# The loads of the residual tile move from SP's queue to ScalarE's, in the output-projection stage of an attention and expert layer

## The chip, the cores and the metric

One Trainium2 chip, eight of its cores. Every core runs the same program on one of the eight sequences (2048 tokens of 1024 numbers); the cores do not exchange data. The time is the device time of the slowest core, in microseconds (us).

## The reference

Two sublayers, each with a layer norm ahead of it and one behind it, and a residual added:

```python
x = x + _layernorm(_L0_attn_ref(_layernorm(x, axis=-1), Wq, Wk, Wv, Wo, ...), axis=-1)
x = x + _layernorm(_L0_ffn_ref(_layernorm(x, axis=-1), router_w1, router_w2, w1, w2, w3), axis=-1)
```

The first is differential attention: eight heads, each with two score matrices, O = (softmax(Q1 K1) - lambda softmax(Q2 K2)) V, an RMS norm of O per head, and `jnp.einsum('bne,de->bnd', O, Wo)`, a projection from 2048 to 1024. The second has 16 experts. Each picks the 256 tokens of the sequence with the highest router probability, computes w3 (silu(w1 x) * (w2 x)) and scatters the weighted results back. The inputs and outputs are float32; the kernel computes its matmuls in bf16.

## The kernel before

The program has five instruction streams, written out in order by a helper, `Plan`: `t` for TensorE, `v` for VectorE, `s` for ScalarE (ACT), `g` for GpSimd and `y` for SyncE (SP). `prod` appends an instruction that raises its engine's counter. `need(e, token)` appends a wait of engine `e` for another engine's counter (L79), but only if `e` has not already waited for that count or a higher one (L77). `dma(q, ...)` appends a load or store to the stream of engine `q` (L85); it is issued when that engine's program arrives at it. `need_dma` waits for the semaphore of a group of transfers (L90). `join_all` makes every engine wait for all others and for all transfers.

The stages, one behind the other and parted by `join_all`: layer norm and transpose of x with attention, head by head (L305 to L572); the output projection with residual and both norms (L576 to L693); the router and the choice of tokens; the experts (loads of w1, w2, w3 in float32, casts, three matmul groups for each of 64 chunks); the scatter with the last norm.

The change is in the output projection. Attention has left its result, transposed, in DRAM (`sc_ot`, 2048 x 2048 bf16), and the transposed Wo in `sc_wot`. SP first issues 16 loads that bring all of Wo to `s_woT` (L585, 256 KB each). Then a loop over `qc`, four blocks of 512 tokens:

- SP issues 16 loads of 128 KB into `s_otq[par]` (L599), one of two buffers. A row of a partition is 512 bf16 values, 1 KB.
- SP issues four loads of 512 KB of the kernel's input x into `s_x4` (L603), each a token tile of 128 x 1024 float32, so rows of 4 KB. There is one `s_x4` buffer; L601 asks that the adds of the block before have read it.
- TensorE waits for the block's `s_otq` loads (L604) and for no others, and does 8 groups of 16 matmuls (L612). VectorE copies each group to `s_ao4` (L622).
- VectorE takes mean and variance (L629 to L638), ACT makes 1/sqrt from it by Ln and Exp (L641, L644), VectorE applies them (L649, where it also waits for the x4 loads, L647, and for the x2 stores of the block before, L648) and adds `s_x4` (L655). The token of the adds is `x4_used`.
- SP waits for the four adds (L659) and stores the sum x2 to DRAM, four stores of 512 KB (L661).
- VectorE and ACT do the second norm (L666 to L684), with its result kept in `s_x2n`. ACT waits for the statistics (L677) ahead of L678, and has nothing behind L681 until L641 of the next block.

SP goes through this in program order. In block `qc + 1` its loads therefore stand behind the stores of block `qc`, and so behind L655 of block `qc`. The name `s_x` in the profile stands for both `s_x4` and `s_x24`, since buffer numbers are left out: `s_x<-x` are the loads that the change touches, `sc_x<-s_x` the stores of x2.

Of the kernel before, what the change touches and what calls it, by code (L numbers as in the profile page):

```python
# [125 lines left out]
def build_program(cfg):  # L126
    nc = bass.Bass("TRN2", target_bir_lowering=False)
    T, H, E, DFF, D = cfg.tok, cfg.heads, cfg.experts, cfg.dff, cfg.d
# [76 lines left out]
    p = Plan(nc)  # L205
# [12 lines left out]
    ds_xr = [p.dma_sem(f"ds_xr{i}") for i in range(2)]  # L218
# [84 lines left out]
    xre = x_in.ap().rearrange("(n p) f -> n p f", p=128)  # L303
# [275 lines left out]
    s_x4 = sb("s_x4", [128, 4 * D], F32)  # L579
# [11 lines left out]
    x4_used = None  # L591
# [3 lines left out]
    for qc in range(NQ):  # L595
        par = qc % 2
        p.need("y", otq_used[par])
        for ec in range(2 * H):
            p.dma("y", s_otq[par][:, ec * 512:(ec + 1) * 512],  # L599
                  sc_ot.ap()[ec * 128:(ec + 1) * 128, qc * 512:(qc + 1) * 512], ds_otr[par])  # L600
        p.need("y", x4_used)  # L601
        for i in range(4):
            p.dma("y", s_x4[:, i * D:(i + 1) * D], xre[qc * 4 + i], ds_xr[0])  # L603
        p.need_dma("t", ds_otr[par])  # L604
        evs = []
        for qt in range(4):
# [51 lines left out]
        x4_used = ad_toks[-1]  # L658
# [624 lines left out]
```

How the kernel before makes its waits and increments, by code:

```python
    def prod(self, e, fn):  # L60
        self.cnt[e] += 1
        lvl = self.cnt[e]
        s = self.sem[e]
        self.ops[e].append(lambda eng, fn=fn, s=s: fn(eng).then_inc(s, 1))
        return (e, lvl)
# [1 line left out]
    def need(self, e, *tokens):  # L67
        for tok in tokens:
            if tok is None:
                continue
            pe, lvl = tok
            if pe == e:
                if self.waited[e][e] < lvl:
                    self.ops[e].append(lambda eng: eng.drain())
                    self.waited[e][e] = self.cnt[e]
            else:
                if self.waited[e][pe] < lvl:
                    s = self.sem[pe]
                    self.ops[e].append(lambda eng, s=s, L=lvl: eng.wait_ge(s, L))
                    self.waited[e][pe] = lvl
# [1 line left out]
    def dma(self, q, out_ap, in_ap, ds, **kw):  # L82
        ds.issued += 16
        self.ops[q].append(
            lambda eng, o=out_ap, i=in_ap, s=ds.sem, kw=kw: eng.dma_start(o, i, **kw).then_inc(s, 16))
# [1 line left out]
    def need_dma(self, e, ds):  # L87
        lvl = ds.issued
        if lvl and self.dma_waited[e].get(id(ds), 0) < lvl:
            self.ops[e].append(lambda eng, s=ds.sem, L=lvl: eng.wait_ge(s, L))
            self.dma_waited[e][id(ds)] = lvl
```

## Time and profile before

| | |
|---|---|
| median of 2 runs | 5681.36 us (5604.35 and 5758.37) |
| the profiled execution | 5599.2 us, its span 5597.3 us on the slowest core |
| TensorE matmuls busy | 2713.5 us (48%) |
| weight loads (PEld) busy | 1725.8 us (31%) |
| VectorE busy | 1631.3 us (29%) |
| ScalarE busy | 1142.9 us (20%) |
| DMA, mean over the span | 82 GB/s, 457.00 MB |
| the largest entry of the chain that ended last | the expert loads `s_wf<-w`, 21% |
| the stage of the change | from 2292.9 to 2558.8 us of the span |

The busy shares are averages over stages that have different limits. No engine is busy for even half of the span. The chain that ended last goes from the last instruction back to what released it, step by step; it shows which kind of work, in which line, the time passed through. Rows of engine PE are matmuls, of PEld weight loads, SPq and ACTq are the issuing of transfers by SP and by ACT. A DMA issue by `Plan` has the line of the helper, L85, whatever line called it, so it is told by its tile names.

### The profile page before, as it was taken

To read this page: it belongs to the slowest core of one execution; us is meant where nothing else is said; L and a number is where in the kernel's file an instruction comes from. 1 tells how busy PE (TensorE), PEld (TensorE's weight loads), DVE (VectorE), ACT (ScalarE), POOL (GpSimd) and SP (SyncE) were. 2 spreads that over 40 slices of the span, in tenths; PEclk is the share of its full clock that TensorE was granted. 3 is DMA by queue.
4 is the path that set the end of the run, shared out by engine and by line. 5 is a ranking of instruction groups with operands and counts; after the bars stand their busy time and mean duration, and the time that the engine had idled before them with its cause. 6 is when DMAs were issued, how large, how long until landed. Compare 5 with 4: busy or idle time off the path is not lost.

```text
span 5597.3 us, 51906 instructions; the slowest of 8 cores (5546.0 to 5597.3 us)
## 1 busy us (share of the span) xinstructions
PE 2713.5 (48%) x16889; PEld 1725.8 (31%) x16889; DVE 1631.3 (29%) x4599; ACT 1142.9 (20%) x1987; POOL 36.9 (1%) x70
## 2 busy tenths in 40 slices
PE   0055646555655665351002555555455555546555
PEld 0033334333433443220001333333334433333222
DVE  1133333323233333341383112222122222213343
ACT  0024334242524334100000111111111111110000
POOL 0000000000000000000000000000000000000000
PEclk9987777877877787675555777777778887778888
DMA  1120110101011000331002665656666566661010
GB/s 46 50 65 19 34 47 5 46 6 45 6 45 33 19 14 6 106 100 33 12 0 72 159 169 163 180 159 163 164 163 166 155 184 169 162 165 34 31 38 34
DMA packets 205642, 457.00 MB, mean 82 GB/s; under 512 B 98596, under 2 KB 107078, under 8 KB 197190
## 3 DMA queue, kind: packets, MB, share of 16 engines
q1 hardware_dynamic: 148902, 218.52, 12.8%
q10 hardware_dynamic: 46080, 167.79, 10.1%
q0 software_dynamic: 10400, 67.38, 6.6%
q8 instruction: 144, 2.36, 0.2%
q14 instruction: 116, 0.95, 0.1%
HBM read 474.67 MB, written 29.36 MB: 90 GB/s over the span
## 4 chain that ended last, share of the span: by engine, by line
PE 36%; DMA 29%; DVE 15%; SPq 8%; ACT 6%; issue 4%; DVEq 2%; ACTq 1%
DMA s_wf<-w 21%; PE pO L502 9%; SPq L85 8%; PE pS L1176 5%; ACT s_w2c L938 3%; DMA s_otT<-s_otil 3%; PE pO L976 2%; PE pQ L385 2%; PE pQ L1044 2%; PE pQ L509 2%; DVE s_m L784 2%; PE pA L509 2%; DVEq L74 2%; PE pA L385 1%; DVE s_ohs L1164 1%
## 5 line engine op out<-in xcount | busy, mean ns | idle before, releaser
L502 PE MATMUL pO<-s_v,s_et 128*128 128x257 bf16 x4096 | 630.1, 286 | 422.1 <-ACT s_et L493 409.7
L938 ACT ACTIVATE s_w2c<-s_wf 128x1024 bf16<-128x1024 f32 x256 | 270.3, 1056 | 1694.5 <-DMA s_wf<-w 1694.5
L502 PEld LDWEIGHTS pO<-s_v,s_et 128*128 128x128 bf16 x4096 | 416.7, 102 | 612.5 <-issue 474.4
L1044 PE MATMUL pQ<-s_xgT,s_w2c 128*128 128x256 bf16 x1024 | 199.2, 376 | 755.3 <-ACT s_gs L1060 755.3
L1044 PEld LDWEIGHTS pQ<-s_xgT,s_w2c 128*128 128x128 bf16 x1024 | 130.9, 131 | 813.7 <-issue 767.3
L493 ACT ACTIVATE s_et<-pQ,s_bias 128x512 bf16<-128x512 f32 x512 | 336.8, 691 | 75.5 <-PE pQ L479 54.3
L493 ACT ACTIVATE s_et<-pA,s_bias 128x512 bf16<-128x512 f32 x512 | 338.1, 693 | 12.1 <-PE pA L509 10.9
L385 PE MATMUL pQ<-s_xnT,s_wqT 128*128 128x512 bf16 x256 | 77.1, 469 | 525.7 <-DVE s_woTh L349 284.0
L924 DVE CAST s_w1c<-s_wf 128x1024 bf16<-128x1024 f32 x256 | 173.0, 691 | 542.8 <-DMA s_wf<-w 542.6
L1176 PE MATMUL pS<-s_ye,s_ohs 128*128 128x512 bf16 x1024 | 263.3, 403 | 117.3 <-DVE s_ohs L1164 117.3
L518 DVE COPY s_o<-pO 128x257 f32<-128x257 f32 x256 | 91.0, 418 | 659.2 <-PE pO L502 659.2
L976 PE MATMUL pQ<-s_ohg,s_x2n 128*128 128x256 bf16 x512 | 103.8, 286 | 356.8 <-DVE s_ohg L958 311.4
L1094 PE MATMUL pO<-s_w3c,s_hb 128*128 128x512 bf16 x1024 | 248.6, 399 | 44.6 <-DVE s_hb L1079 44.6
L1079 DVE TENSOR_TENSOR s_hb<-pQ,s_gs 128x256 bf16<-128x256 f32 x128 | 52.7, 422 | 667.4 <-PE pQ L1044 654.4
L385 PEld LDWEIGHTS pQ<-s_xnT,s_wqT 128*128 128x128 bf16 x256 | 29.0, 116 | 571.4 <-issue 555.9
L1176 PEld LDWEIGHTS pS<-s_ye,s_ohs 128*128 128x128 bf16 x1024 | 95.0, 101 | 240.8 <-issue 158.9
L976 PEld LDWEIGHTS pQ<-s_ohg,s_x2n 128*128 128x128 bf16 x512 | 50.7, 101 | 371.8 <-issue 364.6
L976 PE MATMUL pO<-s_ohg,s_x2n 128*128 128x256 bf16 x1024 | 162.4, 284 | 0.0
L509 PE MATMUL pQ<-s_qt,s_kt 128*128 128x512 bf16 x384 | 161.3, 420 | 0.0
L1164 DVE COPY s_ohs<-pT 128x128 bf16<-128x128 bf16 x512 | 79.1, 217 | 273.2 <-PE pT L1155 273.2
L1094 PEld LDWEIGHTS pO<-s_w3c,s_hb 128*128 128x128 bf16 x1024 | 103.4, 102 | 168.4 <-issue 71.6
L279 ACT ACTIVATE s_col<-s_col 128x1 f32<-128x1 f32 x32 | 6.5, 203 | 709.1 <-DVE s_col L277 709.1
(200 smaller groups left out, 3843.3 us busy)
## 6 DMA issues: line engine op xcount, KB each, us to landing
s_wf<-w ACTq DMA_DIRECT2D x256, 512.0 KB, 5.1
s_wf<-w SPq DMA_DIRECT2D x256, 512.0 KB, 6.5
s_w3c<-w POOLq DMA_DIRECT2D x64, 1024.0 KB, 11.8
s_xstage<-x SPq DMA_DIRECT2D x16, 512.0 KB, 3.6
s_wsf<-wq ACTq DMA_DIRECT2D x16, 512.0 KB, 4.3
s_wsf<-wk ACTq DMA_DIRECT2D x16, 512.0 KB, 5.5
s_wsf<-wv ACTq DMA_DIRECT2D x16, 512.0 KB, 4.8
s_wsf<-wo ACTq DMA_DIRECT2D x16, 512.0 KB, 4.7
```

The source lines that it names most:

```text
L85: lambda eng, o=out_ap, i=in_ap, s=ds.sem, kw=kw: eng.dma_start(o, i, **kw).then_inc(s, 16))
L385: ins = t.matmul(bank[:], wbuf[:, j * 256 + et * 128: j * 256 + et * 128 + 128], s_xnT[:, j * T + qc * 512: j * T + (qc + 1) * 512], start ...
L493: texp = p.prod("s", lambda s, kt=kt, bi=bi: s.activation(s_et[:, kt * 512:(kt + 1) * 512], pAb[bi][:], AF.Exp, bias=s_bias[:], scale=SCAL ...
L502: return t.matmul(pO[qt][:, 0:257], s_et[:, kt * 512 + qt * 128: kt * 512 + qt * 128 + 128], s_v[:, kt * 257:(kt + 1) * 257], start=(kt == ...
L509: return t.matmul(pAb[bi][:], s_kt[:, half * T + kt2 * 128: half * T + (kt2 + 1) * 128], s_qt[:, half * T + qc * 512: half * T + (qc + 1) ...
L924: tok = p.prod("v", lambda v, qtr=qtr, par=par, buf=buf: v.tensor_copy(s_w1c[par][:, qtr * 1024:(qtr + 1) * 1024], s_wf1[buf][:]))
L938: tok = p.prod("s", lambda s, qtr=qtr, par=par: s.activation(s_w2c[par][:, qtr * 1024:(qtr + 1) * 1024], s_wf2[:], AF.Copy))
L976: ins = t.matmul(gbanks8[dt][:, 0:256], s_x2n[:, tt * D + dt * 128: tt * D + dt * 128 + 128], s_ohg[:, tt * 256:(tt + 1) * 256], start=(tt ...
L1044: g_ins = t.matmul(fb[f][:, 0:256], wc[par][:, f * 1024 + j * 128: f * 1024 + j * 128 + 128], s_xgT[:, j * 256:(j + 1) * 256], start=(j == ...
L1094: ins = t.matmul(pO[2 * st + dc][:, 0:512], s_hb[:, f * 256 + st * 128: f * 256 + st * 128 + 128], s_w3c[par][:, f * 1024 + dc * 512: f * ...
L1164: tev.append(p.prod("v", lambda v, k4=k4, par=par: v.tensor_copy(s_ohs[par][:, k4 * 128:(k4 + 1) * 128], pT[:, k4 * 128:(k4 + 1) * 128])))
L1176: ins = t.matmul(scat_banks[bi][:], s_ohs[par][:, (st * 2 + ts_) * 128:(st * 2 + ts_ + 1) * 128], s_ye[:, e * 2048 + st * 1024 + dc * 512: ...
```

## The change

In the loop over blocks of 512 tokens, the wait for `x4_used` and the four loads of `s_x4` are appended to ACT's stream and not to SP's. Their place in the text of the program is the same: behind the `s_otq` loads of the block and ahead of its matmuls. The semaphore, `ds_xr[0]`, the sizes and the readers are the same.

```diff
         for ec in range(2 * H):
             p.dma("y", s_otq[par][:, ec * 512:(ec + 1) * 512],
                   sc_ot.ap()[ec * 128:(ec + 1) * 128, qc * 512:(qc + 1) * 512], ds_otr[par])
-        p.need("y", x4_used)
+        p.need("s", x4_used)
         for i in range(4):
-            p.dma("y", s_x4[:, i * D:(i + 1) * D], xre[qc * 4 + i], ds_xr[0])
+            p.dma("s", s_x4[:, i * D:(i + 1) * D], xre[qc * 4 + i], ds_xr[0])
         p.need_dma("t", ds_otr[par])
```

## Rows read from the trace of the kernel before

**Rows 1.** Spans and granted TensorE clock of the cores: the shortest and the longest.

```profile
core 0: 5546.0 us, clock 0.776
...
core 2: 5597.3 us, clock 0.771
```

**Rows 2.** Busy by stretch, one per block: length, PE, PEld, DVE, ACT, POOL, PEclk, DMA share, GB/s.

```profile
2292.90:2360.80 67.90, 29.35 (x128) 12.80 (x128) 18.75 (x32) 0.96 (x8) 0.00 (x0) 0.73 0.41 124
2360.80:2422.50 61.70, 29.17 (x128) 12.76 (x128) 27.34 (x52) 2.03 (x16) 0.00 (x0) 0.75 0.32 102
2422.50:2486.10 63.60, 30.37 (x128) 13.10 (x128) 27.34 (x52) 1.92 (x16) 0.00 (x0) 0.71 0.31 99
2486.10:2558.80 72.70, 29.57 (x128) 12.88 (x128) 35.92 (x72) 2.88 (x24) 0.00 (x0) 0.71 0.34 116
```

**Rows 3.** Chain that ended last, 2280 to 2570: start us, us, what; the line first.

```profile
by line: PE pQ L612 21.8%; SPq L85 21.5%; PE pA L612 19.1%; DMA s_otq<-sc_ot 6.8%; DVE s_x L655 4.8%; DVEq L74 3.8%; issue 3.6%; DVE s_bn L629 3.4%; DVE s_x L649 3.1%; DVE s_bn L631 2.5%; DMA s_otT<-s_otil 1.6%; DMA sc_ot<-s_otT 1.2%; DVE s
...
2372.73 4.54 DMA s_otq<-sc_ot
...
2434.38 5.31 DMA s_otq<-sc_ot
```

**Rows 4.** Waits in 2280 to 2570, engines' and SP's: total us, times, longest us.

```profile
PE pQ L612 <- DMA s_otq<-sc_ot: 148.1, 4, 49.7
...
SPq L79 <- DVE s_x L655: 190.6, 16, 45.0
```

**Rows 5.** Timeline, block 0: start us, us, engine, line, what, [idle before it <- releaser].

```profile
2292.87 8.59 SPq L85 DMA_DIRECT2D s_woT<-sc_wot  x16
2301.50 9.62 SPq L85 DMA_DIRECT2D s_otq<-sc_ot  x16
2311.16 2.15 SPq L85 DMA_DIRECT2D s_x<-x  x4
2315.71 8.63 PE L612 MATMUL pQ<-s_woT,s_otq 128*128 128x512 bf16 x32 [49.72 <-DMA s_otq<-sc_ot]
```

**Rows 6.** Timeline from the adds of block 0 into block 1.

```profile
2351.83 0.48 ACT L641 ACTIVATE s_col<-s_col 128x1 f32<-128x1 f32 x4 [68.86 <-DVE s_col L638]
...
2356.12 4.63 DVE L655 TENSOR_TENSOR s_x<-s_x 128x1024 f32<-128x1024 f32 x4
2360.83 2.86 SPq L85 DMA_DIRECT2D sc_x<-s_x  x4
...
2363.73 9.43 SPq L85 DMA_DIRECT2D s_otq<-sc_ot  x16
...
2367.28 0.64 ACT L681 ACTIVATE s_col<-s_col 128x1 f32<-128x1 f32 x4
...
2373.20 2.13 SPq L85 DMA_DIRECT2D s_x<-x  x4
...
2377.51 8.45 PE L612 MATMUL pQ<-s_woT,s_otq 128*128 128x512 bf16 x32 [32.46 <-DMA s_otq<-sc_ot]
...
2413.45 0.48 ACT L641 ACTIVATE s_col<-s_col 128x1 f32<-128x1 f32 x4 [45.54 <-DVE s_col L638]
```

**Rows 7.** Issues on L85 over the whole span: ns min/median/max, first and last start.

```profile
L85 SPq DMA_DIRECT2D s_otq<-sc_ot x64: 320/433/1212, 2301.5 to 2497.8; - x64
...
L85 ACTq DMA_DIRECT2D s_wsf<-wk x16: 334/334/362, 281.0 to 1811.3; - x16
```

**Rows 8.** Busy time by stretches in block 0, columns as in rows 2.

```profile
2293.00:2296.00 3.00, 0.00 (x0) 0.00 (x0) 0.00 (x0) 0.00 (x0) 0.00 (x0) 0.50 0.65 191
2302.00:2317.00 15.00, 1.29 (x4) 0.49 (x5) 0.00 (x0) 0.00 (x0) 0.00 (x0) 0.50 1.03 313
```

**Rows 9.** The same around the loads of block 1.

```profile
2361.00:2368.00 7.00, 0.00 (x0) 0.00 (x0) 5.44 (x16) 1.07 (x8) 0.00 (x0) 0.50 0.89 318
2368.00:2374.00 6.00, 0.00 (x0) 0.00 (x0) 2.98 (x4) 0.00 (x0) 0.00 (x0) 0.50 0.83 225
```

**Rows 10.** Tile s_otq, all 64 loads of the stage: us from issue to landing.

```profile
DMA to landing us min/median/max: 2.8/4.2/7.8
```

## The prediction

> **What bounds the kernel now.** I read the per-core spans first [rows 1]: the eight cores lie between 5546.0 and 5597.3 us at one clock, so the slowest core stands for all. The page's chain of work that ended last is spread over the expert loads, attention and the scatter; the edited loop is one short stage of it. The table of engine times by stretch [rows 2] cuts that stage into its four blocks of 512 tokens: 67.9, 61.7, 63.6 and 72.7 us, 265.9 us or 4.8% of the span. Whatever the edit does, it acts there. Each block has TensorE busy for about 29 us and idle for the rest.
>
> The chain inside the stage [rows 3] says why a block is twice as long as its matmuls: the parts are serial. The order is matmuls (L612, 41% of this stretch with both tile names), VectorE's normalisation, then SP issuing loads (21.5%), then the landing of the last `s_otq` load (6.8%), then matmuls again. The waits [rows 4] agree: TensorE waits 148.1 us, four times, for `s_otq`, and nothing in the stage waits for `s_x4`. SP in its turn waits up to 45 us at a time for L655, because the x2 stores stand in its order ahead of the next block's `s_otq` loads. So two things set a block's start: when the `s_otq` loads are issued, and how quickly the 16 DMA engines move them once issued.
>
> **What the edit takes away.** Four issues of `s_x4` per block, 16 in all, leave SP's order. On SP they stand behind the 16 `s_otq` issues, not ahead of them [rows 5, 6]: in block 0, otq from 2301.50 and x4 from 2311.16; in block 1, otq from 2363.73 and x4 from 2373.20. The issues cost 2.15 and 2.13 us, but after them SP has nothing to do until the adds at L655 of that block end, over 40 us later [rows 4, 6]. Saved on the path: 0. The wait that moves with them is no instruction on either engine. The helper `need` drops a wait on a count that the engine has already waited past. SP has waited for all four adds before its x2 stores (L659); ACT has waited for a later VectorE count (L677) before its last activations of a block. Nothing is queued behind a new wait, since there is none. Price 0.
>
> **What it adds on ACT.** Four issues at the place where ACT's program stands: for block 0 right behind the join, at about 2293, for blocks 1 to 3 behind the last activation of the block before (L681, in block 0 at 2367.28 and 0.64 long, so from 2368.0). ACT's issues of loads of the same 512 KB take 0.334 us at the median elsewhere in this kernel [rows 7], so 4 × 0.334 = 1.3 us. Behind them on ACT is L641, which comes at 2351.83 in block 0 and 2413.45 in block 1 [rows 6]: 45 us of cover. If that cover were gone, the price would be 1.3 us a block. VectorE, which reads `s_x4` at L655 (2356.12 in block 0), has even more cover against a late arrival. Price 0.
>
> **What it moves: the time at which 2.1 MB per block enter the DMA engines.** This is the only term with a size. Today x4 follows `s_otq` and is hidden under the matmuls. After the change it enters before or amid `s_otq`.
>
> Block 0. The DMA share is 1.03 from 2302 until 2317 [rows 8], while the end of `s_woT` (4.2 MB in all) and `s_otq` (2.1 MB) pass. The engines are full, so anything put ahead delays the end of `s_otq` by its own transfer time. The rate in this stretch is 313 GB/s. So x4 takes 2.097 MB / 313 GB/s = 6.7 us. The share of 0.65 in 2293 to 2296 leaves 0.35 × 3 = 1.0 us idle, part of which only is start-up latency and can be used: I take 0.5 off. x4 is issued within 2 us and 6.3 MB of other loads are there to share with, so under any fair sharing it is through before the last `s_otq`. **+6.2 us**; bounds 0 (x4 always yields) and 6.7.
>
> Blocks 1 to 3. ACT issues from 2368.0, SP is at that moment half-way through its `s_otq` issues (2363.73 + 9.43 = 2373.16). Bytes: 7 us at 318 GB/s from 2361 to 2368 [rows 9] make 2.23 MB, the x2 stores being 2.10 of it, so 1.97 MB of `s_otq` are still to come. They come at 225 GB/s and a share of 0.83 (2368 to 2374), so in 1.97 MB / 225 GB/s = 8.8 us, for which full engines would need 0.83 × 8.8 = 7.3 us. x4 needs 6.7 us. Its first byte comes some 1.5 us after the issue (my choice, about half of the shortest landing, 2.8 us [rows 10]). Then three ways:
> - x4 goes through first or gets the larger part: 7.3 + 6.7 − 8.8 = +5.2 us;
> - both get the same bytes: from 2369.5, the remaining 1.97 − 1.5 × 0.225 = 1.63 MB of `s_otq` at 150 GB/s, about half of 313, take 10.9 us instead of 1.63 MB / 225 GB/s = 7.2: +3.7 us;
> - x4 yields: 0.
>
> I take 5.0, nearer the first: a row of x4 is 4 KB and one of `s_otq` 1 KB, so turns taken row by row would give x4 four bytes in five. **+15 us** for three blocks. Sum: 0 + 0 + 6.2 + 15 = **+21 us**. The profiled execution lasted 5599.2 us (its span 5597.3 and 1.9 around it), so 5620.4; I say **5620**. The bounds of the sum are 5599.2 and 5599.2 + 6.7 + 3 × 6.7 = 5626. That base stands 82 us below the median of the two runs shown, 5681.36, and 5 us below the lower of them.
>
> The shared engines are also a matter of the Trainium skill (DMA: Bandwidth & Descriptors, "Issuing engines are not separate DMA queues"): loads issued from different engines run on the same 16 DMA engines and interleave, and only the issue time is saved. By it the edit saves SP's 8.6 us of issue, which lie on no path here. The same page ("Queues, rings and completion order") has each DMA engine take turns between queues, a packet of several descriptors at a time; by that rule x4 gets the larger part and the sum is 6.2 + 3 × 5.2 = +22 us. The trace of before shows no two queues with rows of unlike size at once, so it doesn't decide this.
>
> **The rivals.**
> - *x4 yields, or finds enough gaps* (the change does nothing measurable): the queue of SP, which has up to 16 issues waiting, keeps the engines, x4 slips behind. For it: the share is 0.83 while SP is issuing [rows 9], so there is some room. Against: the room is 8.8 − 7.3 = 1.5 us of 6.7, and in block 0 there is none. Time: 5599 to 5607.
> - *A small gain*: in blocks 1 to 3 the last `s_otq` load lands 4.5 to 5.3 us after its issue [rows 3], above this stage's minimum of 2.8 [rows 10], and the x4 loads issued right behind it may be a cause. If moving them cured that without putting their bytes in the way: 3 × 2 = −6 us, 5593. Against: the bytes have to pass somewhere, and they are issued earlier, not later.
> - *SP's issues stretch* (the other side: slower by more than the forecast). An SP issue in this stage takes 0.433 us at the median but up to 1.212 [rows 7]. If x4 in the other queue held all 16 issues of each block at 1.2, a block would start 16 × 0.77 = 12 us later: +49 us, 5648. For it: such rows exist. Against: in block 0 the engines are full throughout and SP still issues 16 in 9.62 us, 0.60 each [rows 5]. It would decide the verdict only from 112 / 4 = 28 us a block, that is 1.75 us more on each issue, which no row comes near.
> - *ACT late for the normalisation*: 45 us of cover, no chance worth a number.
>
> **How the numbers follow.** Contention as summed, +12 to +27 us: 0.62. x4 yields: 0.18. Small gain: 0.07. SP's issues stretch, +27 to +60: 0.07. Something that none of the rows shows: 0.06. The first four lie within 2% of 5599 (112 us), about what a measurement of this kernel can tell from no change; to pass it the stage, 266 us, would have to change by two fifths. So only the last 0.06 can fall outside, and I give more of it to slower, since the known term has that sign: faster 0.02, slower 0.04, same 0.94. For the range the mechanism gives 5593 to 5626 for nine tenths of the chance, but executions of one kernel differ by more than that: the two shown are 5604.35 and 5758.37. At the low end I take 5590; at the high end the shown median with my term on it, 5681 + 21 = 5702. The likeliest case's own range is 5605 to 5635.
>
> **What would show it.** In the profile after: four ACTq rows `s_x<-x` at about 2293, 2368 and so on; the rows of engine time with a DMA share near 1.0 where 0.8 stood; TensorE's wait for `s_otq` up from 148.1 to about 169 us; the first matmul of block 0 some 6 us later after the `s_woT` issues begin (now 22.8 us, then about 29), of blocks 1 to 3 some 5 us later after the end of L655 (now about 16.8, then about 22); the four x4 loads landing in 7 us or more; no change anywhere outside the stage. If the wait stays at 148 us, x4 yields. If the otq issues take 16 × 1.2 us, the third rival holds. The forecast is wrong if the stage gets shorter, or if TensorE's first matmul moves by over 7 us a block.

## The result

| | before | after |
|---|---|---|
| median | 5611.48 us (42 runs) | 5638.3 us (43 runs) |
| the profiled execution | 5599.2 us | 5626.89 us |
| span, slowest core | 5597.3 us | 5625.0 us |
| span, mean over the eight cores | 5565.9 us | 5598.4 us |
| ratio | | 1.0057, 95% interval 1.0038 to 1.0077 |

The kernel became slower by 0.57%, which is 0.0057 × 5611 = 32 us, with an interval of 21 to 43 us. Each kernel has some executions that are disturbed, up to 4% longer and at a lower TensorE clock; the ratio leaves them out, the medians don't. The prediction named 5620 us and a range of 5590 to 5702 that holds the median of 5638. But 5620 is below the 5681.36 that was then the median of two runs, so read against it the number forecast a gain, and there was a loss. What the text priced, +21 us on a profiled execution of 5599.2, has the right sign and is at the lower edge of what was measured.

The stage in its four blocks, as [rows 2], from the table of engine times by stretch of the kernel after:

```profile
2297.30:2374.20 76.90, 30.44 (x128) 13.05 (x128) 18.75 (x32) 0.96 (x8) 0.00 (x0) 0.68 0.37 109
2374.20:2443.30 69.10, 29.66 (x128) 12.89 (x128) 27.33 (x52) 2.01 (x16) 0.00 (x0) 0.72 0.30 91
2443.30:2514.20 70.90, 30.42 (x128) 13.09 (x128) 27.33 (x52) 1.92 (x16) 0.00 (x0) 0.69 0.30 89
2514.20:2593.90 79.70, 29.41 (x128) 12.82 (x128) 35.92 (x72) 2.88 (x24) 0.00 (x0) 0.69 0.32 106
```

Read the first number of each row: 76.90, 69.10, 70.90 and 79.70 where [rows 2] has 67.90, 61.70, 63.60 and 72.70. The busy times of the engines move by 1.1 us at most; the blocks got 7 to 9 us longer, nearly all of it in idle time. The waits of the kernel after name it, as [rows 4]:

```profile
ACT s_col L641 <- DVE s_col L638: 238.7, 4, 77.9
...
PE pQ L612 <- DMA s_otq<-sc_ot: 177.4, 4, 57.6
```

TensorE waits 177.4 us where it waited 148.1. This is core 2, the slowest in both profiles, and it is at the upper end: over the eight cores the wait was 146.1 to 151.5 before (mean 148.4) and 165.5 to 177.9 after (mean 172.4). So +24.0 us on the mean and +29.3 on core 2. The timeline of block 0 and the start of block 1 after, as [rows 5, 6]:

```profile
2296.85 2.25 ACTq L85 DMA_DIRECT2D s_x<-x  x4
2297.30 11.94 SPq L85 DMA_DIRECT2D s_woT<-sc_wot  x16
2309.29 12.73 SPq L85 DMA_DIRECT2D s_otq<-sc_ot  x16
2327.98 9.72 PE L612 MATMUL pQ<-s_woT,s_otq 128*128 128x512 bf16 x32 [57.62 <-DMA s_otq<-sc_ot]
...
2374.20 2.85 SPq L85 DMA_DIRECT2D sc_x<-s_x  x4
2377.09 12.78 SPq L85 DMA_DIRECT2D s_otq<-sc_ot  x16
...
2380.85 0.33 ACTq L85 DMA_DIRECT2D s_x<-x  x1
2380.86 0.37 ACT L681 ACTIVATE s_col<-s_col 128x1 f32<-128x1 f32 x3
2381.22 2.43 ACTq L85 DMA_DIRECT2D s_x<-x  x3
...
2397.83 8.94 PE L612 MATMUL pQ<-s_woT,s_otq 128*128 128x512 bf16 x32 [39.40 <-DMA s_otq<-sc_ot]
```

ACT issues x4 ahead of `s_woT` in block 0 and 4 us into the `s_otq` issues in block 1, as was foretold. From the first `s_woT` issue to the first matmul it is 30.7 us on this core, 22.8 before. From the first x2 store to the first matmul of block 1 it is 23.6 us, 16.7 before. SP's 16 `s_otq` issues now take 12.8 us and not 9.4.

### The profile page after: what moved, and what is told of

Same layout as the page of the kernel before. It is cut to its first block, busy times and chain, and to the rows that moved or that the text cites. A ratio compares the mean times of both kernels' runs of the same rounds, so it can differ in the third digit from the quotient of the medians.

```text
span 5625.0 us, 51906 instructions; the slowest of 8 cores (5585.2 to 5625.0 us)
## 1 busy us (share of the span) xinstructions
PE 2714.4 (48%) x16889; PEld 1723.0 (31%) x16889; DVE 1631.7 (29%) x4599; ACT 1142.6 (20%) x1987; POOL 36.3 (1%) x70
## 4 chain that ended last, share of the span: by engine, by line
PE 35%; DMA 29%; DVE 15%; SPq 9%; ACT 6%; issue 4%; DVEq 2%; ACTq 1%
DMA s_wf<-w 21%; PE pO L502 9%; SPq L85 9%; PE pS L1176 4%; ACT s_w2c L938 3%; DMA s_otT<-s_otil 3%; PE pO L976 2%; PE pQ L385 2%; PE pQ L509 2%; PE pQ L1044 2%; DVE s_m L784 2%; DVEq L74 2%; PE pA L509 2%; PE pA L385 1%; DVE s_ohs L1164 1%
## 5 line engine op out<-in xcount | busy, mean ns | idle before, releaser
L1176 PE MATMUL pS<-s_ye,s_ohs 128*128 128x512 bf16 x1024 | 263.4, 403 | 117.1 <-DVE s_ohs L1164 117.1
L1176 PEld LDWEIGHTS pS<-s_ye,s_ohs 128*128 128x128 bf16 x1024 | 95.0, 101 | 241.0 <-issue 159.2
L612 PE MATMUL pQ<-s_woT,s_otq 128*128 128x512 bf16 x256 | 65.3, 420 | 177.4 <-DMA s_otq<-sc_ot 177.4
```

Source lines behind the costliest of these rows:

```text
L1176: ins = t.matmul(scat_banks[bi][:], s_ohs[par][:, (st * 2 + ts_) * 128:(st * 2 + ts_ + 1) * 128], s_ye[:, e * 2048 + st * 1024 + dc * 512: ...
```

## The experiments

The stage is short against the scatter of whole runs, so most experiments are read by two sizes from their profile that this scatter hardly touches, averaged over the eight cores: TensorE's wait for `s_otq`, and the **lags**. In block 0 the lag goes from the first `s_woT` issue to the first matmul, in blocks 1 to 3 from the first issue of an x2 store to the first matmul of the next block. The stage runs from the first `s_woT` issue to the first transpose of the router.

| kernel | wait us | lags us, blocks 0 to 3 | stage us |
|---|---|---|---|
| before | 148.4 | 23.1, 16.9, 16.9, 17.1 | 266.9 |
| before, second profile | 150.0 | 24.1, 17.2, 17.1, 17.2 | 268.4 |
| after | 172.4 | 28.6, 22.8, 23.2, 23.3 | 291.3 |
| after, second profile | 170.8 | 28.2, 22.4, 22.8, 23.0 | 289.7 |
| x4 on ACT, behind the landing of `s_otq` | 144.9 | 22.7, 16.1, 15.9, 15.8 | 263.4 |
| x4 on SP, ahead of `s_otq` | 170.2 | 29.3, 22.4, 22.2, 21.9 | 288.3 |
| only block 0's x4 on ACT | 153.0 | 28.0, 17.0, 17.0, 16.7 | 271.2 |
| x4 on ACT in rows of 1 KB | 170.4 | 30.1, 22.2, 21.6, 22.0 | 289.0 |
| one x4 load of four | 153.0 | 24.1, 18.2, 18.0, 18.2 | 272.6 |
| two x4 loads of four | 159.2 | 25.7, 19.8, 19.4, 19.9 | 276.6 (cores 0 to 3) |
| `s_otq` one block ahead, x4 on SP | 51.0 | | 208.6 |
| `s_otq` one block ahead, x4 on ACT | 57.3 | | 214.8 |

**The changed kernel again**, without an edit.

> The changed kernel again, beside the other kernels of this group. The measure is TensorE's wait for s_otq, summed over the four blocks and averaged over the eight cores: 148.4 us before, 172.4 us in the profile after. Every theory expects the same again, 172 us within 5, and a time some 0.4 to 0.8% above before.

The wait was 170.8 us and the stage 289.7. Its timed runs gave no ratio.

**The place in time and not the queue.** Two edits take the two apart. The first leaves x4 on ACT and lets ACT wait for the landing of the block's `s_otq`:

```diff
+        p.need_dma("s", ds_otr[par])
         p.need("s", x4_used)
         for i in range(4):
             p.dma("s", s_x4[:, i * D:(i + 1) * D], xre[qc * 4 + i], ds_xr[0])
```

> The four x4 loads stay on ACT, but ACT waits for the block's s_otq loads to land before it issues them. Theory (bytes: x4's 2.1 MB pass the DMA engines ahead of the end of s_otq, whichever engine issues them): the cost goes away whole, wait 146 to 150 us, time as before within 0.2%. Rival (the second queue costs by itself, by switching between queues or by ACT's issues): a good part of the 24 us stays, wait above 158. Rival (small gain: x4 issued right behind s_otq on the same queue slows its last load today): wait 141 to 145, below before.

The second leaves x4 on SP, and issues it ahead of the `s_otq` loads:

```diff
+        p.need("y", x4_used)
+        for i in range(4):
+            p.dma("y", s_x4[:, i * D:(i + 1) * D], xre[qc * 4 + i], ds_xr[0])
         for ec in range(2 * H):
             p.dma("y", s_otq[par][:, ec * 512:(ec + 1) * 512],
                   sc_ot.ap()[ec * 128:(ec + 1) * 128, qc * 512:(qc + 1) * 512], ds_otr[par])
-        p.need("y", x4_used)
-        for i in range(4):
-            p.dma("y", s_x4[:, i * D:(i + 1) * D], xre[qc * 4 + i], ds_xr[0])
```

> The kernel before with the four x4 loads on SP ahead of the 16 s_otq loads, so the same order of bytes with only one queue. Theory (bytes): 2.1 MB in full engines at about 290 GB/s are 7.2 us a block, wait 148 + 29 = 177 us, at least as much as in the changed kernel. Rival (second queue costs by itself): x4 ahead on the same queue costs only the room-corrected 5 us a block or less, wait 160 to 169, below the changed kernel.

The wait with x4 late on ACT was 144.9 us, with x4 early on SP 170.2. So the whole cost goes with the time of issue: it is gone with ACT as issuer, and it is there with SP as issuer. The ratio to before of the late version was 0.9991 (0.9962 to 1.0019), no difference. From the timeline of the late version (core 2; one line was added, so L612 is L613 here), and from that of the early one (core 2):

```profile
2363.47 9.68 SPq L85 DMA_DIRECT2D s_otq<-sc_ot  x16
2376.44 1.78 ACTq L85 DMA_DIRECT2D s_x<-x  x4
2376.62 9.44 PE L613 MATMUL pQ<-s_woT,s_otq 128*128 128x512 bf16 x31 [31.82 <-DMA s_otq<-sc_ot]
```

```profile
2375.73 2.86 SPq L85 DMA_DIRECT2D sc_x<-s_x  x4
2378.64 3.44 SPq L85 DMA_DIRECT2D s_x<-x  x4
2382.12 10.68 SPq L85 DMA_DIRECT2D s_otq<-sc_ot  x16
2398.93 8.67 PE L612 MATMUL pQ<-s_woT,s_otq 128*128 128x512 bf16 x31 [38.97 <-DMA s_otq<-sc_ot]
```

In the first, ACT's issues stand beside TensorE's start and the `s_otq` issues keep their 0.6 us each. In the second, SP's 16 issues take 10.68 us though no second queue is at work; in block 0 of the same core they took 13.18. So longer issues come with x4's bytes ahead of them and not with the second queue. A full share alone doesn't bring them: in block 0 of the kernel before it is 1.03 [rows 8] and the 16 issues take 9.62 us.

The late version's lags in blocks 1 to 3 are also 1.0 us shorter than those of before, and its wait 3.5 us (5.1 against the second profile of before). Issued right behind `s_otq`, as in the kernel before, x4 delays the last loads a little. That is the "small gain" rival's mechanism, at about half of the 2 us a block that it was given (1.0 us, and 1.2 against the second profile of before); no timed run resolves it.

**Only block 0.** x4 on ACT in block 0, on SP in the others.

```diff
-        p.need("y", x4_used)
+        xq = "s" if qc == 0 else "y"
+        p.need(xq, x4_used)
         for i in range(4):
-            p.dma("y", s_x4[:, i * D:(i + 1) * D], xre[qc * 4 + i], ds_xr[0])
+            p.dma(xq, s_x4[:, i * D:(i + 1) * D], xre[qc * 4 + i], ds_xr[0])
```

> Only block 0's x4 loads on ACT, the other blocks' on SP as before. All theories: block 0 starts its matmuls later and the others don't. Bytes theory: block 0's matmuls begin 30 us after the first s_woT issue (22.8 before, 30.7 after), the other three blocks begin 16.8 to 17.5 us after the end of their adds as before; wait 148 + 7 = 155 us. If blocks 1 to 3 were slowed by a state that block 0 leaves behind, they would show more than 18 us.

Block 0's lag was 28.0 us (23.1 and 24.1 before), that of the other blocks 16.7 to 17.0, as before. The blocks pay one by one. Block 0 pays 4 to 5 us over the mean of the cores, not the 7 that core 2 had suggested.

**The size of the price.** Three kernels change what x4 moves. Half:

```diff
-        for i in range(4):
+        for i in range(2):
             p.dma("s", s_x4[:, i * D:(i + 1) * D], xre[qc * 4 + i], ds_xr[0])
...
-            s_x4[:, i * D:(i + 1) * D])) for i in range(4)]
+            s_x4[:, (i % 2) * D:(i % 2 + 1) * D])) for i in range(4)]
```

> The changed kernel with two of the four x4 loads in each block (left out: the loads of two token tiles; the adds read the two that were loaded twice). Theory (price by bytes): half of the 24 us, wait 148 + 12 = 160 us. Rival (a fixed price for a second queue starting, seen as a stretch of 2 us at 54 GB/s behind ACT's issue in block 1 of the changed kernel): the price falls by less than half, wait 164 to 170.

A quarter, the same edit with 1 for 2:

> The changed kernel with one of the four x4 loads in each block (left out: three token tiles' loads; the adds read the one that was loaded). Theory (price by bytes): a quarter, wait 148 + 6 = 154 us. Rival (fixed price of the second queue): wait 160 us or more. With half and whole this gives the price at three sizes, so a straight line and where it meets zero bytes.

All of it, in rows of 1 KB:

```diff
         for i in range(4):
-            p.dma("s", s_x4[:, i * D:(i + 1) * D], xre[qc * 4 + i], ds_xr[0])
+            for c in range(4):
+                p.dma("s", s_x4[:, i * D + c * 256: i * D + (c + 1) * 256],
+                      xre[qc * 4 + i][:, c * 256:(c + 1) * 256], ds_xr[0])
```

> The changed kernel with x4 in 16 loads of 256 columns, so rows of 1 KB as s_otq has, and the same bytes. Theory (x4 gets through whole before the end of s_otq): the price doesn't fall, wait 170 us or more. Rival (turns by row: with rows of 4 KB x4 gets four bytes in five, with rows of 1 KB one in two): blocks 1 to 3 pay about 3.7 us instead of 5 or more, wait 160 to 166.

One load: 153.0 us. Two loads: 159.2 over all cores, 158.0 on cores 0 to 3, which have 154.4 with one load and 171.7 with four. Four loads: 172.4 over all cores. From one to four loads the wait grows by (172.4 − 153.0) / 3 = 6.5 us a load. The line passes two loads at 159.5, and it meets zero loads at 146.5, between the late version (144.9) and before (148.4). So no fixed price for a second queue shows; the price goes by bytes. A load in each of four blocks is 2.1 MB, and 2.1 MB / 6.5 us = 323 GB/s, about the rate of full engines (313 GB/s in [rows 8]). With the second profile of after, 170.8, it is 5.9 us a load, so the price is known to about a tenth.

Rows of 1 KB changed the wait little, 170.4. In blocks 1 to 3 the lag is 1.2 us shorter on the mean, in block 0 it is 1.5 longer. Yet the size of the rows does decide how the two queues share the engines. The DMA view splits packets and bytes by queue, q1 for SP's and q10 for ACT's. These are six microseconds of block 1 on core 2 in which both carry loads (packets, MB, share), 2385 to 2391 of the changed kernel and then 2380 to 2386 of the one with rows of 1 KB:

```profile
q10 hardware_dynamic: 388, 1.44, 81.1%
q1 hardware_dynamic: 349, 0.32, 20.1%
```

```profile
q1 hardware_dynamic: 750, 0.68, 51.0%
q10 hardware_dynamic: 727, 0.66, 44.8%
```

The two queues pass about equal numbers of packets, so the bytes go by the size of the rows: 4.5 to 1 with rows of 4 KB against 1 KB, 1 to 1 with equal rows. Over all cores and blocks 1 to 3, from 11 to 15 us behind the first x2 issue, it is 4.2 to 1 (3.2 to 5.5) and 1.0 to 1 (0.9 to 1.1). The price hardly follows because nearly all of x4 has passed by the time of the first matmul in either kernel: of the 6.30 MB of x2 stores, `s_otq` and x4, 6.30 and 6.25. The test isn't clean: 16 issues in place of 4 also spread x4 over a longer time.

**`s_otq` one block ahead.** The experiments say that a block's start hangs on what SP issues when. So the loads of block qc+1, for which the second buffer is free, were put ahead of the wait for block qc's adds:

```diff
     for qc in range(NQ):
         par = qc % 2
-        p.need("y", otq_used[par])
-        for ec in range(2 * H):
-            p.dma("y", s_otq[par][:, ec * 512:(ec + 1) * 512],
-                  sc_ot.ap()[ec * 128:(ec + 1) * 128, qc * 512:(qc + 1) * 512], ds_otr[par])
+        if qc == 0:
+            load_otq(0)
         p.need("y", x4_used)
...
         p.need_dma("t", ds_otr[par])
+        if qc + 1 < NQ:
+            load_otq(qc + 1)
```

(`load_otq(b)` holds the removed lines for block b.)

> The kernel before with SP's order changed: the s_otq loads of block qc+1 are issued behind x4 of block qc and ahead of the x2 stores of block qc. Theory (the start of blocks 1 to 3 hangs on SP's order and the loads behind it): TensorE's wait for s_otq falls to block 0's part, about 50 us; VectorE's normalisation, 26 us a block, becomes the bound together with four groups of matmuls. Saved 12 to 20 us a block, in all 40 to 60 us, ratio 0.989 to 0.993. Rival (the loads move the wait to the copies or to the DMA engines, where they meet the stores): under 20 us saved.

> The kernel with s_otq one block ahead and x4 on SP, again with more timed rounds, since the interval was wide. Stage 266.9 before and 208.6 here make 58 us of 5600: ratio 0.989 to 0.991 by the theory that nothing outside the stage changes. If other stages gain too, below 0.987.

And the same with x4 on ACT, at the places of the changed kernel:

> The s_otq loads one block ahead, ahead of the x2 stores, as in the kernel that had 51.0 us of wait and a stage of 208.6 us (mean over the cores) with x4 on SP; here x4 is on ACT, at the places of the changed kernel. Theory (the edit costs only where s_otq is awaited behind x4's bytes): blocks 1 to 3 no longer pay, block 0 still does: wait 55 to 58 us, stage 212 to 216 us. Rival (x4 on ACT costs by itself in each block): stage 225 us or more.

With x4 on SP the wait fell to 51.0 us and the stage from 266.9 to 208.6, in both profiles. The first timing gave a wide 0.984 (0.9687 to 0.9993), the second 0.9919 (0.9896 to 0.9941). With x4 on ACT: wait 57.3, stage 214.8, ratio 0.9908 (0.9881 to 0.9936). Both beat both kernels. The second ratio is a little weaker than was foretold (0.989 to 0.991): over the cores the mean span fell by 42 us, the stage by 58. The waits of the version with x4 on SP (core 4; L612 is L620 and L622 is L630 here):

```profile
DVE s_ao L630 <- PE pQ L620: 68.8, 10, 39.1
...
PE pQ L620 <- DMA s_otq<-sc_ot: 52.4, 1, 52.4
PE pQ L620 <- DVE s_ao L630: 39.1, 4, 13.2
```

TensorE waits for `s_otq` once, in block 0. In the other blocks it waits for VectorE to free a PSUM bank, 13 us each. There x4 on ACT costs nothing: the two versions differ by 6.2 us in the stage and 6.3 in the wait, which is block 0's price alone. The same edit costs 24 us or 6 us, by what is being waited for beside it.

**What lies outside the stage.** Over the cores the mean span grew by 32.5 us from the profile before to that after, and the stage by 24.4. Of the rest, 9 us are in the expert stage (from the first issue of an `s_wf` load to that of the first load of the scatter, `s_xstage<-sc_x`), where the code is the same: 2030.5 us before, 2039.8 after and 2040.5 in the second profile of after.

> The kernel before once more, with a profile. The question is the expert stage, where the code is the same: 2030.5 us (mean over the cores) in the profile of before, 2039.7 and 2040.5 in two profiles of the changed kernel. If this is scatter between executions, some execution of before lies at 2035 or more and some of the changed kernel below it; if it follows from the edit, before stays at 2031 within 2 and the changed kernel at 2040.

> The changed kernel a third time, for the same question: the expert stage at 2040 us again if it follows from the edit, anywhere between 2029 and 2041 if it is scatter. The stage of the edit 290 us and TensorE's wait 171 us, both within 4.

Before came out at 2030.9 again. The third profile of the changed kernel is of an execution of 5815.6 us, with 307.6 us in the stage of the change; it can't be set against the others here. Its wait was 172.6. But the two profiles of the kernel with `s_otq` ahead, one and the same program, have 2034.5 and 2041.0; only block 0's x4 on ACT has 2039.3, x4 early on SP 2028.7, and x4 on ACT in rows of 1 KB, with about the wait of the changed kernel, 2032.3. Executions of one program thus differ by 6.5 us there, and the 9 us do not go with the wait. Whether the edit has a part in them stays open.

## Why the prediction was right or wrong

- **Nothing is gained on SP, no wait is added, ACT has room.** Right. The issues behind `s_otq` were on no path: with x4 off SP and late, the time is the same. ACT's next work still comes 53 us later ([rows 6] has 45).
- **The term is contention in the DMA engines.** Right, and shown from both sides: same queue and early costs 22 us, other queue and late costs nothing, and the price goes by bytes.
- **Block 0, +6.2 us.** Measured 5.5 over the cores, 7.9 on core 2; 4.1 between the two second profiles, and 6.3 where `s_otq` goes one block ahead. Right within that scatter.
- **Blocks 1 to 3, +5.0 us each.** Too low: 5.9, 6.4 and 6.2 over the cores, 6.9 to 7.2 on core 2. The step that failed in the sum is the credit for room, "7.3 + 6.7 − 8.8". It held the engines to be 17% free while SP issues `s_otq`, and x4 to fill that. The stretch from the first x2 issue to the first matmul of block 1, of the kernel before and then of the kernel after (columns as in [rows 2]), shows that it doesn't:

```profile
2360.83:2377.51 16.68, 0.00 (x0) 0.03 (x1) 8.59 (x20) 1.07 (x8) 0.00 (x0) 0.50 0.87 276
```

```profile
2374.20:2397.83 23.63, 0.00 (x1) 0.03 (x1) 8.58 (x20) 1.05 (x8) 0.00 (x0) 0.50 0.87 267
```

  The DMA share is 0.87 in both, so the engines' idle time grew, from 2.2 to 3.1 us, where the credit had it shrink by 1.5. Over the cores and blocks 1 to 3 it was 2.0 us before, 3.4 after and 3.2 with x4 late. Where it lies is seen in the rows of the kernel after behind ACT's issue:

```profile
2381.00:2383.00 2.00, 0.00 (x0) 0.00 (x0) 1.66 (x3) 0.23 (x3) 0.00 (x0) 0.50 0.64 54
...
2386.00:2389.00 3.00, 0.00 (x0) 0.00 (x0) 0.00 (x0) 0.00 (x0) 0.00 (x0) 0.50 1.04 287
```

  In the first row no byte of x4 moves yet: its first packet came 2.6 us after ACT's issue on the mean of the cores (the text chose 1.5). The kernel before has such a dip too, 6 to 8 us behind its first x2 issue (0.77 and 145 GB/s from 2367 to 2369); whether ACT's issues deepen it is not shown. Once x4's packets flow, the share is 1.0, and x4 has landed 2.7 us ahead of the last `s_otq`. So the room lies ahead of x4 and behind it, and x4 pays its whole time. The straight price, 2.1 MB at 313 GB/s = 6.7 us a block, gives +27 us. The four lags add up to 24 against the kernel before and to 27 against the late version, since x4 behind `s_otq` costs 3 us in the kernel before, which the sum had at nothing.
- **Which of the ways of sharing.** The text leaned on the size of the rows to say that x4 gets four bytes in five. It did, 4.2 bytes to 1, and with rows of 1 KB one in two. The price followed only by 1.2 us a block, near the 1.5 between the text's 5.2 and 3.7, because all or nearly all of x4 has passed before the first matmul either way. As to the Trainium skill (DMA: Bandwidth & Descriptors, "Issuing engines are not separate DMA queues"), which has loads of all issuing engines interleave on the same 16 DMA engines: the runs agree, with 172.4 and 170.2 us of wait from the two queues.
- **The rivals.** "x4 yields" would have left 148 us of wait; it was 172. "A small gain" is real in its cause and worth 3.5 us of wait, but only when x4 comes late. "SP's issues stretch": the median went from 0.433 to 0.643 us on core 2, with single ones of 2.6, but it rises with one queue too, to 0.622. It is not a cost on top: the wait with one queue is the same, and on core 2 the last `s_otq` load of blocks 1 to 3 now lands 9.8 to 10.9 us after its issue, so the issue is not what is late.
- **The number.** This is where the prediction failed as a forecast. The sum was made on the profiled execution's 5599.2 us and was stated as 5620, although the median then shown was 5681. The two are not on one footing: 42 runs of before have a median of 5611.48, 70 us below that of the two and 12 above the profile. An effect of 21 us is far below the first gap and of the order of the second. The sum should have been carried as a difference of +0.4% onto the shown median; the text saw the gap of 82 us, and used it for the range only. Its own sign of being wrong, a first matmul that moves by over 7 us a block, came out on core 2 (7.9, 6.9, 7.2 and 7.2 us) and not on the mean of the cores (6.0).
- **What the sum leaves out.** Of the measured 32 us (21 to 43) the stage explains 24. The rest is within the interval and was not settled.

## What to carry to other kernels

A transfer that is hidden behind the one the engines wait for is hidden by its place, not by its size: issued earlier, from either engine, it cost here its bytes at the rate of full DMA engines. Moving loads to a second queue gives up the order that the single queue kept, and the loads with the longer rows took the larger part of the bytes; if they move, let them wait for the landing of the load that matters. And look first for the load that could be issued ahead: here the next block's `s_otq` was held back by the wait of the x2 stores for their adds, and issuing it ahead of that wait brought 0.8 to 0.9%.

## What the runs showed of the hardware

- The time that SP spends on one issue of a 128 KB load rose when x4's bytes were ahead of it: on core 2 a median of 0.433 us in the kernel before, 0.643 in the kernel after (up to 2.629), 0.622 with x4 early on the same queue, 0.432 with x4 late.
- Two queues at once passed about as many packets each (388 and 349 in 6 us), whatever their size: rows of 4 KB beside rows of 1 KB got 4.2 times the bytes, rows of 1 KB beside rows of 1 KB the same bytes.
- Cores of one program, all at work on the same loads, pay unlike prices, and not always the same cores: in the kernel after, TensorE waited 165.5 us on core 1 and 177.9 on core 3, in its second profile 162.9 on core 4 and 176.9 on core 2; before, the spread was 146.1 to 151.5.
